# Taking the full-array bf16 product ahead of each half step's flips out of the three narrow attention stages

## The reference

```python
# L0_ffn's attention: causal, 256 keys, 16 heads of 8
# L1_attn: 4 x 256 rows, a band mask over the keys, 16 heads of 8
# L1_xattn: 512 context keys, no mask, 16 heads of 8
scores = q @ k.T * scale + mask
p = softmax(scores)          # over the keys
o = p @ v                    # then the output product, added to x
```

## Time and profile before

| | |
|---|---|
| three runs | 2749.92 us median (2747.77 to 2759.25) |
| profiled execution | 2752.27 us, its span 2750.5 us |
| TensorE busy | 2475.0 us, 90% |
| VectorE, ScalarE, GpSimd busy | 1774.7, 1535.7, 1363.7 us |
| granted TensorE clock over the span | 0.943 |

### The profile page before, as it was taken

One profiled execution on the slowest core, in us unless ns is written; L12 is line 12 of the kernel. 1 busy time (PEld: TensorE's weight loads), 2 busy tenths in 40 slices (PEclk: granted clock), 3 DMA queues, 4 the chain that ended last, 5 costly groups with the idle time before them and its releaser, 6 DMA issues. The chain is left out here.

```text
span 2750.5 us, 57927 instructions
## 1 busy us (share of the span) xinstructions
PE 2475.0 (90%) x20585; PEld 1601.9 (58%) x20585; DVE 1774.7 (65%) x4074; ACT 1535.7 (56%) x4979; POOL 1363.7 (50%) x1981
## 2 busy tenths in 40 slices
PE   6899978898989989978558999689999999999997
PEld 3566645555645555646444666356666666666665
DVE  4566655535656755555554555577888788878884
ACT  2456536523746745633224555357766776777664
POOL 0455534301536633320003444488878788788773
PEclk8899998998989999999778999999999999999998
DMA  3000000010000010000010000101010111101000
GB/s 73 1 1 1 1 9 1 13 33 7 2 4 2 1 35 1 1 7 1 8 29 1 1 1 1 61 14 39 25 44 22 35 29 29 37 24 48 21 23 10
DMA packets 45711, 47.85 MB, mean 17 GB/s; under 512 B 11947, under 2 KB 31413, under 8 KB 45430
## 3 DMA queue, kind: packets, MB, share of 16 engines
q1 hardware_dynamic: 45430, 44.18, 5.8%
HBM read 31.05 MB, written 0.52 MB: 11 GB/s over the span
## 5 line engine op out<-in xcount | busy, mean ns | idle before, releaser
L1017 POOL TENSOR_TENSOR l_xattn_probs<-l_xattn_probs,rowinv 128x512 f32<-128x512 f32 x128 | 130.3, 1039 | 400.8 <-DVE rowinv L1029 400.8
L2281 ACT ACTIVATE net_probs<-bank,net_negmax 128x96 f32<-128x96 f32 x768 | 250.9, 339 | 113.0 <-DVE net_negmax L2417 111.7
L1037 DVE TENSOR_REDUCE negmax<-scores 128x1 f32<-128x508 f32 (+4 forms) x512 | 211.1, 465 | 107.0 <-PE scores L919 75.4
L1017 POOL TENSOR_TENSOR lora_probs<-lora_probs,rowinv 128x508 f32<-128x508 f32 (+1 forms) x256 | 149.5, 617 | 222.4 <-DVE rowinv L1029 222.4
L2335 POOL TENSOR_TENSOR net_rope<-net_rope,net_sin_parts 128x512 f32<-128x512 f32 x192 | 244.3, 1272 | 9.4 <-DVE net_sin_parts L2387 9.4
L124 DVE COPY turned<-flip 128x512 f32<-128x512 f32 (+3 forms) x280 | 163.3, 583 | 109.7 <-PE heads L972 53.6
L2343 POOL TENSOR_TENSOR net_probs<-net_probs,net_inverse 128x384 f32<-128x384 f32 x192 | 158.7, 827 | 122.3 <-DVE net_inverse L2413 120.4
L2356 POOL TENSOR_TENSOR net_rope<-net_rope,net_head_inv 128x512 f32<-128x512 f32 x192 | 201.2, 1048 | 7.5 <-POOL net_head_inv L1886 0.9
L739 DVE TENSOR_REDUCE negmax<-scores 128x2 f32<-128x256 f32 (+2 forms) x192 | 157.8, 823 | 67.7 <-PE scores L647 38.4
L2417 DVE TENSOR_REDUCE net_negmax<-bank 128x4 f32<-128x384 f32 x192 | 106.4, 554 | 125.7 <-PE bank L2117 123.5
L122 ACT ACTIVATE turned<-flip 128x512 f32<-128x512 f32 (+3 forms) x280 | 143.4, 512 | 73.7 <-PE flip L661 50.9
(11 more groups left out here) (435 smaller groups left out, 6551.0 us busy)
## 6 DMA issues: line engine op xcount, KB each, us to landing
net_w_qkv<-in_L_ffn_Wqkv SPq DMA_DIRECT2D x12, 768.0 KB, 6.0
net_vals_between<-net_vals SPq DMA_DIRECT2D x48, 192.0 KB, 2.5
net_w_out<-in_L_ffn_Wo SPq DMA_DIRECT2D x6, 512.0 KB, 4.2
net_vals_between<-net_vals SPq DMA_DIRECT2D x48, 64.0 KB, 2.0
moe_w<-in_L_ffn_w13T SPq DMA_DIRECT2D x8, 256.0 KB, 2.7
net_w<-in_L_ffn_W SPq DMA_DIRECT2D x6, 341.0 KB
moe_w<-in_L_ffn_w2T SPq DMA_DIRECT2D x8, 128.0 KB, 2.4
ctx_tok<-in_ctx SPq DMA_DIRECT2D x1, 768.0 KB, 6.5
```

Of the source, the lines that this page charges most:

```text
L1017: last = nc.gpsimd.tensor_tensor(own, own, rowinv[:, u * tail + w:u * tail + w + 1].to_broadcast([P, k1 - k0]), ALU.mult)
L1037: last = nc.vector.tensor_reduce(negmax[:, u * tail + w:u * tail + w + 1], scores[:, 2 * qt + h, k0:k1], AX.X, ALU.max, negate=True)
L2281: last = nc.scalar.activation(prob_blocks(g)[:, w, :], score_blocks(g)[:, w // 2, w % 2, :], ACT.Exp, bias=maxima[:, g % 4, w:w + 1], accu ...
```

## The change

The call in the flips is removed with its condition and its constant. Two products a step go, 64 a stage, 192 in all. No other instruction, wait, buffer or order is changed.

```diff
-            QUADS, GROUP, FILL = 4, 4, 1
+            QUADS, GROUP = 4, 4
...
                                         pe.wait_ge(moved[i % 2].sem, moved[i % 2].at(0, 2 * f + half))
-                                    if i == 2 * half:
-                                        keep_warm(flip[:, i % 2, :], FILL)
                                     for k in range(blocks):
                                         last = nc.tensor.transpose(flip[:, i % 2, k * P:(k + 1) * P], probs_of(f, i)[:, k * P:(k + 1) * P],
                                                                    ident[:, :])
```

## The result

The kernel without the fills takes 2846.27 us (median of 5 runs, 2838.13 to 2848.90) against 2749.92 us (2747.77 to 2759.25, by now 5 runs too) before. The ratio, estimated over all the runs and so not quite the quotient of the medians, is 1.0339, 95% interval 1.0322 to 1.0355. It is 96 us slower; 2844 was predicted. All five executions have a mean granted clock of 0.890 to 0.895, where the profiled one before had 0.943: the loss is not an accident of one execution. The profiled execution took 2848.9 us with a span of 2847.1 us, at a clock of 0.891. The spans differ by 2847.1 - 2750.5 = 96.6 us.

A forecast was written before the change was run, and what follows sets the result against it. TensorE's queue was taken to bound the three stages. At a lower clock causal +39, near +57 and cross -2 sum to +94 us; 2752.3 + 94 - 2.4 = 2844 us, 8-in-10 range 2768 to 2860.

The forecast's parts named there:

- TensorE is the bound and other engines have room: In causal, near and cross, TensorE's queue sets each stage's end; other engines have a quarter of the time to spare.
- Nothing swallows the gain: At 2.4 GHz a near step without fills, 3.13 us, still exceeds ScalarE's 2.68 us, so no other engine takes the bound.
- Without fills causal and near stay at 1.2 GHz for most of their length: Likeliest case, causal and near low nearly throughout: +39 us in causal and +57 in near, chance 0.43.
- The inference from the fourth layer's stretch: Fourth layer's self attention, without fills, stayed at 0.50 for 10 us; causal and near without fills should likewise stay low.
- The step lengths: Without fills at 1.2 GHz: near step 5.67 us, two causal steps 9.21; masks to flips 0.12 us at 2.4 GHz.
- A fill's price in cross, 0.12 us: In cross at 2.4 GHz, each removed fill gains 0.12 us, within 0.07 to 0.22, as no masks hide the weight load.
- Cross, -2 us: Cross rises by itself, perhaps a step or two later; fill gains less late steps give -2 us, between -8 and 0.
- The joints: Everything outside the three stages keeps its length, a few us of the clock aside.
- It is the start at 1.2 GHz that matters: Causal and near would keep 2.4 GHz once there; their low start, which no edit touches, decides. No separate size.
- The 39 us: Rival for all three stages: the clock rises as before under continuous work, so removed fills gain 39 us; chance 0.15.
- the first rival: Causal or near recovers 2.4 GHz on the way without fills: +20 to +80 us, 2770 to 2830; chance 0.32.
- Cross did not stay low: Rival: cross too stays at 1.2 GHz, adding 115 us and more, 2960 us; chance 0.05.

The follow-up runs named there:

- the first experiment: Against the kernel before the change, fills kept only in the first six rounds of flips of each stage: 2726.71 us, ratio 0.9897.
- The burst of six: Against the kernel before, causal and near keep only six fills ahead of each half's flips in one mid-stage step, cross none: 2753.74 us, ratio 1.0008.
- the last experiment: Against the kernel before, fills only ahead of stages (six for causal, else twelve) and in the first two steps' waits, none in flips: 2710.09 us, ratio 0.9853.

## Why the prediction was right

- *TensorE is the bound and other engines have room.* Right for the kernel after: it was busy without a gap through each step shown. "Nothing swallows the gain" had been checked on near alone and fails in causal at 2.4 GHz, where two steps take 5.60 us and not 5.19 (the first experiment); causal stood at 1.2 GHz in the kernel after, so the forecast did not feel it.
- *Without fills causal and near stay at 1.2 GHz for most of their length.* Right, to their ends: +40.0 and +56.5 us for the +39 and +57 worked out. This case had been given a chance of 0.43. Near came up only at 879 us, in its last rounds, where no scores are left. The inference from the fourth layer's stretch, where 20 such products followed 10 us at 0.50, held; that layer still reads 0.50 at 1527 us in the kernel after. The burst of six shows the cause directly, and the 32-row fill shows that the rows count, and not occupation alone.
- *The step lengths.* 5.68 us for 5.67 in near; 494.91 - 485.68 = 9.23 for 9.21 in two causal steps; masks to flips 0.19 us at 1.2 GHz, and 719.43 - 719.31 = 0.12 at 2.4 GHz (near of the first experiment), for 0.12. That the flips' weight load hides behind the masks is right.
- *A fill's price in cross, 0.12 us.* Mis-sized. A cross step at 2.4 GHz is 5.17 us in the kernel after against 5.52, so a fill is worth 0.175 us, in the upper half of the 0.07 to 0.22 that was given. The first products of two steps in time order:

```profile
1001.78 1.13 PE L642 MATMUL scores<-kT,qM 32*128 32x512 f32 x4
...
1006.95 1.13 PE L642 MATMUL scores<-kT,qM 32*128 32x512 f32 x4
```

- *Cross, -2 us.* Mis-sized: -9.3, just outside the -8 to 0 given. From the start of the fifth step (838.42 us before, 939.72 after) to the end cross took 163.1 us before and 152.8 after: 10.3 us less for the 60 fills that went, 0.17 each. The forecast had multiplied by 56 and by 0.12. Up to the fifth step it took 1.0 us more although three fills had gone, since the clock rose after 27 us instead of 24; I had put up to two late steps into the term. The rise before had come at 836 us, ahead of the first value products at 837.41 and not with them, so "as its value products began" was read a little wrong. In the kernel after, the scores shrink from 2.08 us to 1.13 behind the first value products:

```profile
933.96 2.08 PE L642 MATMUL scores<-kT,qM 32*128 32x512 f32 x4
...
937.86 1.93 PE L673 MATMUL heads<-turned,dealt_values 128*32 128x128 f32 x32
939.72 1.13 PE L642 MATMUL scores<-kT,cross_q_more 32*128 32x512 f32 x4
```

- *The joints (the time ahead of, between and behind the stages), "a few us".* 96.6 - 87.2 = 9.4 us lie there, 7 of them within what executions of untouched code differ by. The error of cross (-7) and the joints (+9) made up for each other in the sum, so that 2844 came so near to 2846 is luck; that causal and near together were forecast to 1 us is not.
- *"It is the start at 1.2 GHz that matters."* Half right. Once at 2.4 GHz past the first steps the clock of causal and near does hold without fills, in four experiments. But where near and cross entered at 1.00, with twelve fills ahead of them and none after, both lost it in their first steps, so high at the start does not yet mean high afterwards.
- *The rivals.* Continuous work alone does not raise the clock: causal's 130.00 of 130 and near's 150.00 of 150 us ran at 0.50. The Trainium skill ("TensorE: Matmul & The Clock Gate", "Why this matters for your kernels"), by which it should, is not borne out by these rows. The 39 us that it would have gained were mis-sized in two parts that nearly cancel: causal's steps at 2.4 GHz shorten by 0.23 us each and not 0.44, since exponentials come late next (the first experiment's rows), and cross's fills are worth 0.17 us and not 0.12. The delays of 25, 20 and 18 us on which the first rival leaned are nearer to 25, 20 and 24 when cross is counted from its start. Neither stage recovered half way. Cross did not stay low; the 9.6 us worked out for its step at 1.2 GHz is borne out by the last experiment, where two steps start at 798.80 and 808.48 us, 9.68 us apart.

## What to carry to other kernels

A product whose result nobody reads may be what holds TensorE's clock; before one is taken out, look at the granted clock up to and after the first of them, and at what kind of product preceded each rise. Here nearly all of such fills were waste and a few decided 96 us: they cost least where the engine waits anyway, ahead of the stage and in the waits of its first steps, and once the stage's own mix runs at the full clock they can stop (0.9821). A step's length at each of the two clocks, taken from the rows, sized the outcome to 1 us in each of the two stages that stayed low.

## What was unexpected of the hardware

The same stream of instructions runs at either clock and stays there: near's steps stood at 0.50 for 169 us in one experiment, without fills among them, and at 1.00 for 96 in another, with fills in the first few steps of it alone, and TensorE was busy over 98% in both. Full occupation did not bring the clock up; a product on all 128 rows did, the same columns on 32 rows did not, and half the columns on 128 rows did so, in near some 27 us later. It need not be such a fill: 32 transposes alone did it too, and so did cross's own mix of eight transposes to a half step and 32 value products. The other direction surprised too: a stage that began at 1.00 fell after 6 us in which the engine was busy two thirds of the time, and another, busy 8.75 of 10 us, fell too.
